# First expert layer: from every token through every expert to selected rows in blocks of one expert

## What is computed

```python
def _L0_ffn_ref(x, Wg, W1, b1, W2, b2):          # x: 32 x 56 x 128, e = 8 experts, K = 2
    C = 2 * K * T // e                           # T = 1792 tokens, so C = 896 places per expert
    logits = xt @ Wg
    gates = softmax(logits)
    idx1 = argmax(gates); mask1 = one_hot(idx1, e); gate1 = sum(gates * mask1)
    idx2 = argmax(where(mask1 > 0, -inf, logits)); mask2 = one_hot(idx2, e); gate2 = sum(gates * mask2)
    w1, w2 = gate1 / (gate1 + gate2 + 1e-9), gate2 / (gate1 + gate2 + 1e-9)
    pos1 = place of the token among those with the same idx1
    pos2 = place among those with the same idx2, counted behind all first choices of that expert
    keep1, keep2 = pos1 < C, pos2 < C
    xe[idx1, pos1] += xt * keep1;  xe[idx2, pos2] += xt * keep2
    h = gelu(einsum('ecd,edf->ecf', xe, W1) + b1[:, None, :])      # d = 128, f = 512
    ye = einsum('ecf,efd->ecd', h, W2) + b2[:, None, :]
    return ye[idx1, pos1] * (w1 * keep1) + ye[idx2, pos2] * (w2 * keep2)

x = x + _L0_ffn_ref(_layernorm(x), ...)
```

## Time and profile before

| what | value |
|---|---|
| time, median of 3 runs | 1620.69 us (1616.67 to 1622.16) |
| span of the profiled execution | 1623.6 us |
| own device time of the profiled execution | not given apart from its span |
| TensorE busy with matmuls | 1472.4 us, 91% of the span |
| VectorE busy | 1072.5 us, 66% |
| ScalarE busy | 868.7 us, 54% |
| GpSimd busy | 740.0 us, 46% |
| first cross attention, steady steps | about 130 to 329 us of the span |
| first expert part | 328.9 us (first router matmul) to 547.6 us (first projection of the second attention) |
| second attention | 547.6 to about 690 us |

### The profile page before, as it was taken

The page is one execution under the profiler, slowest core; times in us unless marked ns, Lnnn a source line. Parts: engine busy times, 40 slices in busy tenths (PEclk is TensorE's granted clock), DMA queues, the critical chain, the costliest instruction groups (busy, mean ns, idle before and its releaser), DMA issues.

```text
span 1623.6 us, 41089 instructions
## 1 busy us (share of the span) xinstructions
PE 1472.4 (91%) x17024; PEld 943.2 (58%) x17024; DVE 1072.5 (66%) x1732; ACT 868.7 (54%) x1784; POOL 740.0 (46%) x670
## 2 busy tenths in 40 slices
PE   7779999999999899857699999999999999889998
PEld 4557888755444466525466666666666666555554
DVE  6885555533342578686588888888888888635554
ACT  3432333345555333216477777777777777643332
POOL 6673111100000157657478877777877776000000
PEclk9879999999999999969899999999999999989999
DMA  4003000032310231155565655555555554404320
GB/s 120 2 1 107 2 3 2 2 113 60 78 39 13 65 82 39 35 105 104 127 121 131 123 126 128 124 127 126 125 134 123 124 128 106 112 1 94 68 54 17
DMA packets 62540, 129.55 MB, mean 80 GB/s; under 512 B 15794, under 2 KB 38067, under 8 KB 59187
## 3 DMA queue, kind: packets, MB, share of 16 engines
q1 hardware_dynamic: 62354, 126.92, 33.9%
HBM read 100.22 MB, written 26.67 MB: 78 GB/s over the span
## 4 chain that ended last, share of the span: by engine, by line
PE 34%; POOL 10%; ACT 8%; DVE 3%; issue 2%; DMA 1%; SPq 0%; ACTq 0%; POOLq 0%; DVEq 0%
PE ps L1780 8%; PE ps L865 7%; POOL ARENA L1984 7%; PE ps L1764 5%; POOL ARENA L1990 3%; PE ps L877 3%; PE ps L1727 3%; ACT ARENA L1934 3%; PE ps L1718 2%; ACT ARENA L1912 2%; PE ps L1741 2%; ACT ARENA L1925 1%; ACT ARENA L1918 1%; DVE ARENA L1854 1%; PE ps L1789 1%
## 5 line engine op out<-in xcount | busy, mean ns | idle before, releaser
L1854 DVE TENSOR_REDUCE ARENA<-ps 112x2 f32<-112x1000 f32 x384 | 456.5, 1197 | 117.8 <-PE ps L1741 114.6
L1934 ACT ACTIVATE ARENA<-ps 125x448 f32<-125x448 f32 x768 | 378.5, 549 | 129.2 <-PE ps L1764 128.5
L1984 POOL TENSOR_TENSOR ARENA<-ARENA 64x500 f32<-64x500 f32 x192 | 263.8, 1374 | 106.0 <-ACT ARENA L1912 87.5
L107 POOL TENSOR_TENSOR rs<-rs,mhalf 128x1 f32<-128x1 f32 x96 | 57.8, 602 | 371.2 <-DVE rs L102 370.9
L865 PE MATMUL ps<-XT,ARENA 128*128 128x448 f32 x544 | 222.9, 555 | 0.0
L1764 PEld LDWEIGHTS ps<-ARENA 64*125 64x125 bf16 x3072 | 122.4, 134 | 133.5 <-ACT ARENA L1934 70.0
L1764 PE MATMUL ps<-ARENA 64*125 64x112 bf16 x3072 | 169.4, 228 | 19.7 <-ACT ARENA L1934 18.6
L1780 PE MATMUL ps<-ARENA 125*17 125x112 f32 x6144 | 186.2, 261 | 0.0
L865 PEld LDWEIGHTS ps<-XT,ARENA 128*128 128x128 f32 x544 | 105.6, 196 | 100.8 <-issue 100.6
L1741 PE MATMUL ps<-ARENA 64*112 64x500 bf16 x768 | 152.4, 386 | 10.4 <-DVE ARENA L1854 10.4
L877 PE MATMUL ps<-ARENA 128*128 128x448 f32 x400 | 161.6, 539 | 0.0
(11 more groups left out here) (228 smaller groups left out, 2099.7 us busy)
## 6 DMA issues: line engine op xcount, KB each, us to landing
ARENA<-key_parts SPq DMA_DIRECT2D x192, 187.5 KB, 4.4
ARENA<-in_ctxT SPq DMA_DIRECT2D x96, 250.0 KB, 3.8
key_parts<-ARENA SPq DMA_DIRECT2D x64, 375.0 KB, 2.8
ARENA<-token_weights SPq DMA_DIRECT2D x32, 512.0 KB, 5.5
ARENA<-in_L_ffn_W SPq DMA_DIRECT2D x1, 2048.0 KB, 9.7
ARENA<-query_parts SPq DMA_DIRECT2D x6, 192.0 KB, 6.9
ARENA<-in_c_ones SPq DMA_DIRECT2D x2, 562.5 KB, 14.7
ARENA<-in_L_attn_a SPq DMA_DIRECT2D x2, 512.0 KB, 5.3
```

The source lines that it names most:

```text
L1854: e.tensor_reduce(mxp[0:112, b % 2, 2 * g:2 * g + 2, ch], ps[0:112, b1:b1 + 2, 0:500], AX, ALU.max) \
L1934: e.activation(Pb[0:KT, n % NP_, 448 * h:448 * h + 448], ps[0:KT, b1[h], 0:448], ACT.Exp, bias=0.0, scale=1.0).then_inc(exped.sem, 1)
L1984: e.tensor_tensor(T2[r:r + 64, :], T0[64 - r:128 - r, n % 2, :], sin[64 - r:128 - r, sl], ALU.mult) \
```

## The change

Only the rows that were chosen go through an expert. The 16 tiles are split in two halves of 8 (`SPLIT`). For each half the kernel counts how many rows each expert gets, gives each expert whole blocks of 128 rows, and works out a row number for each (token, choice), `IDX`, and for each block which expert it belongs to, `TAB`. GpSimd scatters the normalised rows to a DRAM tensor `slots` by `IDX` with one indirect DMA for each tile and choice; SP loads the blocks back. There are at most 21 blocks in a half (`SLOTS`), 42 in all, and all 42 are always run. For each block TensorE turns the rows, VectorE copies the weights of the block's expert (1156 columns: W1, W2, b1, b2) to one of four places `WT`, at an address that it reads from `TAB` into a register, and the block is an item: 4 matmuls up with 128 columns, 4 Gelu with 128 columns, 4 matmuls down with 128 columns, a sum with the bias on VectorE. SP stores the result to a DRAM tensor `results`; GpSimd gathers by `IDX` the two rows of each token, and VectorE adds them to `XR` with their weights (`combine`).

The first half's routing, scatter and first two blocks move into the steps of the first cross attention (`early_*`), and so do the position sums (`angles`, now in pieces of 2048 columns). The second half's gathers and norms move into the second attention (`LATE_GATHER`, `LATE_NORM`). The core of the diff:

```diff
+SPLIT = ((0, 8), (8, 16))
+SLOTS = tuple((2 * 112 * (b - a) + 8 * 127) // 128 for a, b in SPLIT)
+PADS = 256
...
-                for t in range(NT + 2):
+                early = stages[2].parts["early_pe"]
+                for t in range(NT + 1):
                     if t < NT:
                         scores(t)
                     if 1 <= t <= NT:
                         turn(t - 1)
+                    early(e, w, t, "turned")
...
+            REC = 1156
+            NI = sum(SLOTS)
...
+            def load_slots(e, w, c):
+                w.wait_ge(*scattered[c](2 * (SPLIT[c][1] - SPLIT[c][0])))
+                w.wait_ge(*tabled(1))
+                for d, (lo, hi) in enumerate(parts_of[c]):
+                    if c:
+                        w.wait_ge(*x_turn(sum(g[0] == 0 and g[1] < hi for g in groups)))
+                    e.dma_start(XSB[:, lo:hi], XS[c][128 * lo:128 * hi].rearrange("(i p) d -> p i d", p=128)) \
+                        .then_inc(xs_in[d].sem, 16)
...
+            def early_pe(e, w, t, at):
+                if at == "turned" and t == 10:
+                    route(e, w, 0)
+                if at == "turned" and t == 12:
+                    count(e, w, 0)
+                if at == "last" and t == NT - 1:
+                    turn_slots(e, w, 0)
+                    turn_slots(e, w, 1)
+                    up(e, w, 0)
+                if at == "turned" and t == NT:
+                    up(e, w, 1)
+                if at == "applied" and t == NT:
+                    down(e, w, 0)
...
+            norm_at = {SLOTS[0] + 6 + 2 * j: j for j in range(8)}
...
             def pe(e, w):
+                for i in range(2, NI + 1):
+                    if i < NI:
+                        up(e, w, i)
+                    down(e, w, i - 1)
+                    for g in turned_at(i):
+                        turn_slots(e, w, g)
+                    if i == 2:
+                        ln_turn(e, w, 2, NT - 1, 5, free)
+                    if i == 4:
+                        route(e, w, 1)
+                    if i == 7:
+                        count(e, w, 1)
+                    if i in norm_at:
+                        ln_turn(e, w, 3, norm_at[i], 5, free)
+                stages[3].parts["front_pe"](e, w)
+
+            def copy_weights(e, w, i):
...
+                if i >= 4:
+                    w.wait_ge(*down_mm(i - 3))
+                    w.wait_ge(*y_cp(i - 3))
+                v = nc.values_load(TAB[0:1, i:i + 1], engines=[mybir.EngineType.DVE], min_val=0, max_val=7,
+                                   skip_runtime_bounds_check_because="a count over eight experts, at most seven by its minimum")
+                e.tensor_copy(WT[:, i % 4, :], recs[:, bass.ds(v * REC, REC)]).then_inc(w_cp.sem, 1)
+
+            def result(e, w, i):
...
+                e.tensor_tensor(Y[:, i % 8], ps[:, 2 + i % 2, 0:128], WT[:, i % 4, 1028:1156], ALU.add).then_inc(y_cp.sem, 1)
...
+            def combine(e, w, t):
+                c, j = divmod(t, 8)
+                w.wait_ge(*kept(11))
+                w.wait_ge(*gathered[j](2 * c + 2))
+                for k in range(2):
...
+                    e.scalar_tensor_tensor(XR[:, t, :], xT[:, 256 * j + 128 * k:256 * j + 128 * k + 128], GW[:, t, k:k + 1], XR[:, t, :],
+                                           ALU.mult, ALU.add).then_inc(combine_mul.sem, 1)
...
+                steps = {5: ("logits", "first"), 6: ("second",), 8: ("counts", "bases"), 9: ("slots",), 10: ("table",),
+                         11: ("gates",), 12: ("shares",)}
+                for i in range(1, NI + 1):
+                    result(e, w, i - 1)
+                    if i + 3 < NI:
+                        copy_weights(e, w, i + 3)
...
+            def scatter(e, w, c, n):
+                lo, hi = SPLIT[c]
+                t, k = divmod(n, 2)
...
+                e.indirect_dma_start(XS[c], bass.IndirectOffsetOnAxis(IDX[:, lo + t, k:k + 1], 0), XN[:, lo + t, :], None) \
+                    .then_inc(scattered[c].sem, 16)
...
+            def early_pool(e, w, t):
+                if t in (13, 14):
+                    for n in range(8 * (t - 13), 8 * (t - 13) + 8):
+                        scatter(e, w, 0, n)
 
             def pool(e, w):
-                x_pool(e, w)
...
+                for n in range(16):
+                    scatter(e, w, 1, n)
+                for j in range(10):
+                    if j < 8:
+                        gather(e, w, j)
+                    if j >= 2:
+                        ln_power(e, w, 3, j - 2)
...
+            LATE_GATHER = {0: (8, 9, 10, 11), 1: (12, 13), 2: (14, 15)}
+            LATE_NORM = {1: (8, 9), 2: (10, 11, 12), 3: (13, 14, 15)}
```

785 lines of the change are left out of this document (524 added, 261 removed).

## The result

| | before | changed kernel |
|---|---|---|
| median | 1620.01 us (1616.67 to 1622.16, 4 runs) | 1568.74 us (1567.05 to 1574.22, 4 runs) |
| ratio | | 0.969, 95% interval 0.9668 to 0.9712 |
| span of the profiled execution | 1623.6 us | 1566.1 us |

The account below looks back on a forecast made before the run. TensorE bounds the kernel before, VectorE the new loop: 341.7 + 114 + 3 = 458.7, first projection at 460.7 instead of 547.6, 86.9 us gained, less 10 in the second attention: 77, span 1546.7, median 1544, range 1505 to 1595.

Parts of the forecast that it names:

- the likeliest case: The forecast itself, VectorE bounding the loop: median 1544 us, own range 1525 to 1560, chance 0.44.
- TensorE, after: Expert loop: 1.98 us of TensorE per new item with its block turn, some 88 us in all.
- VectorE, after: Expert loop: 2.25 us an item, 0.9 of it the register load; 114 us in all, so VectorE bounds.
- TensorE bounds the loop: Rival: register load 0.15 us, VectorE 85 us against TensorE's 88; 25 us less, about 1518; chance 0.17.
- hidden: Second half's scatters in the loop: 24.1 us with landing and loading, wanted some 28 us later, so no wait.
- My last line: Last sign of error, "Beyond it all": a late slots load stops TensorE in the middle of the loop; no size.
- s = 1.2: GpSimd's cost in us for one indirect DMA of 128 rows, the middle between 0.55 and 1.90.
- the rival's 25 us: VectorE's copies and GpSimd hold each other up: loop 19 us longer, second attention 6; about 1568; chance 0.13.
- Work moved into the cross attention: Half the router and a count add 2.9 us there, position sums and sine 3 (0 to 8).
- The first half's slots: Ahead of the loop: TensorE's first block turn waits some 6 us for slots; the loop starts at 341.7.
- Second attention: I add 10 (4 to 25): Start of the second attention: gathers ahead of products make them 8 us late, VectorE's norms partly inside that wait.
- The clock rival: TensorE's clock falls in the loop; at half clock all through 50 us more, 1593; chance 0.06.

Follow-up runs that it names:

- the repeat: The changed kernel once more with no edit (also called again), on the chip of the other follow-up kernels; 1559.64 us, ratio 0.961.
- route_early: Changed kernel with the first half's scatters in runs of 5, 5 and 6 and the second half's choosing two items sooner; 1546.46 us, ratio 0.954.
- loads_behind: Changed kernel with the 23 loads of the second cross attention held until the late gathers have landed; 1563.16 us, ratio 0.964.
- late22: Changed kernel with the second half's gathers two tiles a step behind the product, inverse roots ahead of it; 1555.78 us, ratio 0.959.
- all_three: route_early plus loads_behind plus late22's order, but with the first four gathers ahead of the first product; 1554.54 us, ratio 0.959.

## Why the prediction was right, and where it was not

The forecast, faster, came true, the time, 1568.7, lies in the range of 1505 to 1595, but outside the likeliest case's own range (1525 to 1560). The repeat's 1559.6 lies at its edge. In the repeat's marks, without the held-up steps: item 2 starts 1.7 us later than forecast (343.4), the loop is 9.3 us shorter (109.7 against 119.0), and from the first projection on 32.7 us are lost where I had 10: 22.6 in the first six steps of the second attention, most of the rest in the slower clock near the end (last section). Step by step:

- **TensorE, after**: right. 1.79 us an item and 0.11 for its share of a block's turn (four turns in 0.44 us), against 1.98 forecast.
- **VectorE, after: "so VectorE is the new bound"**: wrong. The step that failed is the register load, taken at 0.9 us and measured at 0.30, and the 0.2 of its register instructions, measured at 0.07. The copy (0.78 forecast, 0.77 measured) and the sum (0.29) were right. VectorE is busy 62.8 of 113 us, not over 90%, and an undisturbed item takes 1.79 us, not 2.9. The Trainium skill (DMA: Bandwidth & Descriptors, Latency and other measured facts) has a floor of about 600 ns for such a load; the 42 loads here lie under it, at 0.30, and the measurement decides. The rival "TensorE bounds the loop" had the loop's mechanism right outside the choosing; its 25 us did not come, for the waits in the next point.
- Why the loop was yet only 4.2 us shorter than forecast, 9.3 in the repeat (the 5.2 between them are hold-ups): with a faster loop, what I had taken as **hidden** was not. "The second half's scatters hidden" counted 11 items of 2.25 us; with items of 1.8 to 2.8 us TensorE stands 8.4 us for the slots (again), and 2.8 when the choosing starts sooner (route_early). The stand costs some 2 us more behind it: from 399.8 to 405.2 the clock is granted at 0.50 (1.2 GHz), where it was 1.00 ahead of the stand, and the next three groups of eight matmuls start 1.9, 1.7 and 1.4 us apart instead of 0.9. The rest in the repeat is waits for norms, 2.5 us for the last one of the cross attention and 4.3 for the first half's, and 2.4 us for the choosing, ahead of the count. My last line named this case, "a slots load that lands so late that TensorE stands still in the middle of the loop", and gave it no price.
- **s = 1.2**: right, 0.96 busy and 0.30 to the next, 1.27 from start to start. Beside VectorE's copies a scatter takes up to 1.62 us, and the second 16 take 23 us instead of 20: the added 3 us for VectorE and GpSimd in each other's way was right, and the rival's 25 us did not come. But the copies are held up too, once: in the repeat one of the first four, which run beside the second eight scatters, takes 2.59 us instead of 0.77 (source view of L1228).

```profile
324.59 4.62 DVE L1228 COPY ARENA<-ARENA 128x1156 f32 x4 [0.56 <-issue]
```

  The Trainium skill (SBUF — State Buffer, Who interferes with whom) tells of an exclusive lock between such copies and GpSimd's descriptor writing; the trace agrees: 0.66 us on a scatter (372.54) that starts 0.08 us behind a copy of 0.77, and 1.8 us on that one copy.
- **Work moved into the cross attention**: forecast 5.9 us, measured 3. The mark of step 14 hardly moved (299.94; 300.18 before), but only because step 1 began 3.2 us sooner in that execution. From the scores of step 1 to those of step 14 it was 158.1 us before and is 161.0 (161.3 in the repeat). The 2.9 us that I had for half the router and a count are right: the step with the router takes 13.95 us, the one with the count 13.14, all others about 12.2; the 3 us for the position sums are not there (0.2). Scores of steps 10 and 11, changed kernel, then before:

```profile
248.49 0.54 PE L608 MATMUL ps<-ARENA 128*128 128x448 bf16 x2
...
262.44 0.54 PE L608 MATMUL ps<-ARENA 128*128 128x448 bf16 x2
```

```profile
251.48 0.54 PE L580 MATMUL ps<-ARENA 128*128 128x448 bf16 x2
...
263.66 0.54 PE L580 MATMUL ps<-ARENA 128*128 128x448 bf16 x2
```

- **The first half's slots**: right. The first block turn waits 7.9 us in the repeat, about the 6 forecast, and its item 2 starts at 343.4, forecast 341.7. In the first profile it starts at 351.6 because of the held-up steps.
- **"Second attention: I add 10 (4 to 25)"**: mis-sized, 23.6 measured. I had counted gathers ahead of the products, 8 us, and let most of VectorE's norms fall into that wait. The products come 14.4 and 7.9 us apart (11.5 and 7.6 forecast), which was nearly right. What the sum put at nothing is that the inverse roots stand behind all these gathers and products in GpSimd's queue, with TensorE's queue behind them: one stand of 10.2 us. Holding the loads alone changes nothing (loads_behind), moving the roots ahead and the first gathers back changes nothing (late22, where the landing beside the loads becomes the wait), and all_three, which keeps the first gathers in front, moves the roots ahead and holds the loads, takes the interval ahead of the fifth projection from 27 to 14 us. Whether that needs the loads held is not shown.
- **The clock rival** did not come: the clock was granted at 0.91 in the loop, 0.94 in the repeat.

That the sum hit its range is in part luck: an item that was too dear on VectorE stands against a second attention and waits for slots that were too cheap, and the range was 90 us wide.

What caused the held-up steps of the first profile stays open. That a run of eight scatters does it, with nothing else needed, is excluded by the repeat, which has the same runs of eight and no hold-up. It would take many executions, and on the chip of the first result, to settle; this wasn't tried.

## What to carry to other kernels

A transfer or a queue that is "hidden behind eleven items" is hidden only at the item's forecast price: work out the cover also for the case that the item is cheap. When work is moved behind a part's border, look at what is already issued at that border (here 23 loads, almost 6 MB) and at what stands behind it in an in-order queue; where two such waits are possible, an edit that mends one may bring the other forward (late22 did), so read the waits again after each edit, before a theory is dropped for want of a gain, and change one thing at a time. And take a second profile before building on a stall that no row explains.

## What the runs showed that I had not expected

- A one-word register load into VectorE's queue takes 0.30 us (299 to 550 ns, 42 loads).
- An indirect DMA of 128 rows of 512 bytes keeps GpSimd 0.96 us and 1.27 from start to start, a plain one of the same bytes 0.56. The direction makes no difference (962 ns median for both in the first profile). Beside VectorE it can take longer: a scatter up to 1.62 us beside a copy, a gather 2.03 us beside a sum of two tiles of 1024 columns (462.90 and 462.85 in the repeat).
- Beside the 23 loads a gather of 64 KB landed up to 15.1 us behind its issue (late22), and within 2.7 us with the loads held (loads_behind).
- Held-up steps: in one of ten profiled executions with scatters, TensorE with nothing to wait for started matmuls in groups 0.4 us apart beside scatters, and VectorE saw finished results up to 8 us late, 16.5 us in all.
- The clock near the end of the second cross attention differs from one execution to the next. Windows of ten us in the first profile and in the repeat at the same place of the program:

```profile
1361.00:1371.00 10.00, 6.92 (x178) 5.20 (x166) 1.79 (x8) 7.27 (x17) 0.60 (x1) 1.00 0.01 3
```

```profile
1350.00:1360.00 10.00, 7.61 (x128) 5.69 (x120) 1.20 (x5) 5.67 (x13) 0.60 (x1) 0.58 0.01 2
1360.00:1370.00 10.00, 8.43 (x130) 6.17 (x130) 0.60 (x3) 4.86 (x12) 0.00 (x0) 0.50 0.01 2
```

Granted 1.00 (2.4 GHz) in the one, 0.50 (1.2 GHz) in the other, behind ten us in which TensorE was busy 75 and 76% of the time at 1.00 in both. From the last scores to the first item of the second expert part it is 40.2 us in the first profile and 48.4 in the repeat. These 8 us come and go between executions of one kernel, and are why the marks A and B, not the spans, were compared above.
